# One-core transformer block in fp32: chunk 0 of the router sent through in the last attention slot, and the first two refinement steps reordered around it

## The reference, cut to what matters

```python
x = x + L0_xattn(layernorm(x), ctx)     # FFT autocorrelation, top-11 shifts, one row per sequence
x = x + L0_ffn(layernorm(x))            # 128 -> 512 -> 128, weights composed from 32 low-rank pairs
x = x + L1_xattn(layernorm(x), ctx)     # plain attention, one head of 128
x = x + L1_ffn(layernorm(x))            # router, 8 experts, 2 iterations

# L1_ffn, per token:
logits = gelu(x @ w_r1 + b_r1) @ w_r2 + b_r2          # router: top 2 of 8 experts
integrated, v = x, 0
for _ in range(2):
    ctx = [integrated, v]
    shared = inl(gelu(ctx @ w_s1 + b_s1) @ w_s2 + b_s2)      # alpha, beta, gate
    routed = weighted sum over the 2 experts of inl(gelu(ctx @ w1[e] + b1[e]) @ w2[e] + b2[e])
    x_next, v_next = sw * shared + (1 - sw) * routed
    halt = sigmoid(gelu(x_next @ w_h1 + b_h1) @ w_h2 + b_h2)
    refined = gelu(x_next @ w_f1 + b_f1) @ w_f2 + b_f2
    integrated += halt * refined * integration_weight
    v = v_next
```

## Time and profile before

| what | value |
|---|---|
| median of 3 runs | 349.97 us (349.29 to 350.16) |
| profiled execution | 348.92 us |
| its span, first to last instruction | 347.1 us |
| mean granted TensorE clock | 0.985 |
| TensorE busy | 317.9 us (92%) |
| VectorE busy | 263.5 us (76%) |
| ScalarE busy | 192.9 us (56%) |
| GpSimd busy | 36.5 us (11%) |

### The profile page before, as it was taken

The page is one execution under the profiler, slowest core; times in us unless marked ns, Lnnn a source line. Parts: engine busy times, 40 slices in busy tenths (PEclk is TensorE's granted clock), DMA queues, the critical chain, the costliest instruction groups (busy, mean ns, idle before and its releaser), DMA issues.

```text
span 347.1 us, 4339 instructions
## 1 busy us (share of the span) xinstructions
PE 317.9 (92%) x1482; PEld 224.9 (65%) x1490; DVE 263.5 (76%) x529; ACT 192.9 (56%) x303; POOL 36.5 (11%) x47
## 2 busy tenths in 40 slices
PE   4989999899899458899899999999999999999995
PEld 4764697555465336567576777767777777776763
DVE  1474844558656776798969988999996996999693
ACT  3410024366936643497877966777556746545743
POOL 0030012122020203103710020000000000000000
PEclk9989999999989899999999999999999999999999
DMA  7999940000000000015263154001001000000001
GB/s 265 428 423 293 313 190 0 0 3 1 0 2 0 0 1 2 0 60 136 48 181 60 62 144 85 16 0 32 0 0 28 5 0 1 32 0 20 12 0 60
DMA packets 13172, 25.20 MB, mean 73 GB/s; under 512 B 608, under 2 KB 9056, under 8 KB 11872
## 3 DMA queue, kind: packets, MB, share of 16 engines
q1 hardware_dynamic: 11712, 20.75, 16.7%
q0 software_dynamic: 1440, 4.19, 6.5%
HBM read 16.55 MB, written 1.05 MB: 51 GB/s over the span
## 4 chain that ended last, share of the span: by engine, by line
PE 74%; DVE 14%; ACT 6%; issue 4%; DMA 1%; DVEq 0%; ACTq 0%
PE ps L1346 70%; DVE ring L1014 1%; PE ps L1444 1%; ACT ring L533 1%; ACT L533 1%; DMA pA<-in_packA 1%; DVE st L801 1%; PE ps L1560 1%; PE ps L1463 1%; DVE wz L1014 1%; DVE a L817 1%; PE ps L1433 1%; DVE ring L948 1%; DVE xtok L1001 1%; DVE ring L956 1%
## 5 line engine op out<-in xcount | busy, mean ns | idle before, releaser
L1346 PE MATMUL ps<-hm_even,ew_hi 128*128 128x512 f32 (+1 forms) x152 | 48.6, 418 | 1.4 <-issue 1.4
L1346 PE MATMUL ps<-hm_odd,ew_hi 128*128 128x512 f32 (+1 forms) x148 | 47.1, 421 | 0.0
L1346 PEld LDWEIGHTS ps<-hm_even,ew_hi 128*128 128x128 f32 (+1 forms) x152 | 26.4, 188 | 6.4 <-issue 1.5
L585 ACT ACTIVATE hid<-ps,pB 128x512 f32<-128x512 f32 x32 | 21.7, 688 | 14.4 <-PE ps L1346 13.8
L1346 PEld LDWEIGHTS ps<-hm_odd,ew_hi 128*128 128x128 f32 (+1 forms) x148 | 25.6, 189 | 5.5 <-issue 0.5
L1346 PE MATMUL ps<-hm_even,ew_lo 128*128 128x512 f32 (+1 forms) x72 | 25.3, 392 | 0.0
L431 POOL TENSOR_TENSOR zz<-zz,mhalf 128x4 f32<-128x4 f32 x12 | 12.4, 1034 | 100.3 <-DVE zz L906 100.3
L1346 PE MATMUL ps<-x_hi,w1x_hi 128*128 128x512 f32 x40 | 18.8, 470 | 4.2 <-DVE xtok L1001 3.6
L1346 PE MATMUL ps<-hm_odd,ew_lo 128*128 128x512 f32 (+1 forms) x64 | 22.3, 394 | 0.0
L1014 DVE SCALAR_TENSOR_TENSOR ring<-ring,pB,hid 128x1024 f32<-128x1024 bf16 x16 | 20.5, 1282 | 0.8
L525 ACT ACTIVATE hB<-ps 128x512 f32<-128x512 f32 x16 | 9.6, 597 | 19.8 <-PE ps L1346 19.8
(11 more groups left out here) (324 smaller groups left out, 757.3 us busy)
## 6 DMA issues: line engine op xcount, KB each, us to landing
ring<-in_fc1b SPq DMA_DIRECT2D x4, 1024.0 KB, 17.2
ring<-in_fc2a SPq DMA_DIRECT2D x4, 1024.0 KB, 7.4
hm_odd<-hm_odd SPq DMA_DIRECT2D x4, 512.0 KB, 3.5
packC<-in_packC SPq DMA_DIRECT2D x1, 1152.0 KB, 9.1
pB<-in_packB SPq DMA_DIRECT2D x1, 1077.0 KB, 8.7
ctxT<-in_ctxT SPq DMA_DIRECT2D x2, 512.0 KB, 6.3
xtok<-in_xtok SPq DMA_DIRECT2D x1, 1024.0 KB, 8.7
xT<-in_xT SPq DMA_DIRECT2D x1, 1024.0 KB, 10.7
```

Of the source, the lines that this page charges most:

```text
L585: act.activation(hid[:, j, :], hid_bank(s, j), ACT.Gelu, bias=W("eb1", j, j + 1)).then_inc(sem("hid"), 1)
L1346: return pe.matmul(out, lhsT, rhs, start=start, stop=stop)
```

## The change

Nothing is added to or taken from the arithmetic: the same matmuls, masks and gelus are issued, in another order and partly in other banks. `route`, `second_exp` and `weigh` run three times (chunk 0; chunks 1 and 2; chunk 3) where they ran twice. In words:

- the splits of `w1x`, `wf1`, `wh1` and `wh2` move from slots 1 (ScalarE) and 2 (VectorE) to slot 0
- the router uses bank 4, that of the feed-forward, in place of bank 7, so `scores` waits for no logits any more; `router1` and `router2` of a slot stand behind its scores
- in slot 3 the route of chunk 0 is worked out and expanded, and three of its hidden tiles are computed; the state's high half for steps 0 and 1 is copied by ScalarE instead of VectorE
- the rest of the last chunk's attention, the router of chunk 2, `expand(1)`, and all of chunk 3's norm and router go between tiles of BETA and GATE of step 0
- all tiles of `hidden(1)` use bank 7, so each waits for the gelu of the one ahead
- `expand_weights(0)` and `expand(2)` go behind GATE of step 0, `hidden(2)` into BETA of step 1, and `weights_1` behind it
- `second_exp(3, 1)` stands between `squashed(1, BETA)` and `refine1(0)`

```diff
@@ banks
-            return (bank[7], bank[7], bank[4], bank[1])[c]
+            return (bank[4], bank[4], bank[0], bank[6])[c]
...
+        def routed(c):
+
+            return (1, 2, 2, 3)[c]
@@ gpsimd
+                if n == LN["att", 3]:
+                    pool.wait_ge(sem("minus_1"), 1)
+                    pool.wait_ge(sem("share"), 1)
+                    weigh(0, 1)
             for n, s in enumerate(MOVED):
...
                 if s == 1:
-                    weigh(2)
+                    weigh(1, 2)
+                if s == 2:
+                    weigh(3, 1)
@@ scalar
+            act.activation(w1x_hi, pB[:, colB["ew1"][1]:colB["ew1"][1] + W1C], ACT.Copy)\
+                .then_inc(sem("w1x_hi"), 1)
             gelus(0, (2, 3))
...
+            for t in range(NCH):
+                a, q = t >= 1, t >= 2
+                if t:
+                    gelus(t, range(FT))
+                if a:
+                    exps(t - 1)
+                if t == 1:
+                    act.activation(swc[:, 0:1], W("sw"), ACT.Exp, scale=-1.0).then_inc(sem("swe"), 1)
+                if t == 3:
+                    second_exp(0, 1)
+                if q:
+                    center_evac(t - 2)
+                if t == 2:
+                    r1_gelu(0)
...
+                    state_high(0)
+
+            act.wait_ge(sem("consts"), 4)
+            expand_evac(0, 2, 3)
+            hidden_gelus(0, (1, 3))
+            r1_gelu(1)
+            hidden_gelus(0, (0,))
+            exps(3)
+            center_evac(2)
+            hidden_gelus(0, (2, HT))
+            state_high(1)
+            r1_gelu(2)
+            squashed(0, BETA)
+            expand_evac(1, 7, 6)
+            hidden_gelus(1, (1,))
+            center_evac(3)
+            hidden_gelus(1, (0, 2))
+            r1_gelu(3)
+            hidden_gelus(1, (3, HT))
+            weights_evac(0, 7, 6)
+            expand_evac(2, 7, 6)
+            state_high(2)
+            squashed(0, GATE)
+            second_exp(1, 2)
...
                 squashed(s, BETA)
+                if s == 1:
+                    second_exp(3, 1)
                 refine1(s - 1)
@@ vector
                 if s == 1:
                     kept(s, 2)
                     high(s, 2)
+                    ln_scale("rt", 3)
                     lower(s, 1)
                     kept(s, 3)
                     high(s, 3)
+                    logits(3)
                     lower(s, 0)
                     state_split(s + 1)
                     slot_masks(s + 1)
                     shared_halves(s)
+                    route(3, 1)
...
+                if t == 3:
+                    state_split(0)
+                    route(0, 1)
+                if a:
+                    att_norm(t - 1)
                 if q:
                     ln_scale("rt", t - 2)
...
+            kept(0, 1)
             att_scores(3)
             att_max(3)
+            att_add(2)
+            logits(1)
+            lower(0, 1)
             ln_stats("rt", 2)
+            kept(0, 3)
+            att_norm(3)
+            lower(0, 3)
+            att_pt(3)
             ln_scale("rt", 2)
             kept(0, 2)
             lower(0, 2)
+            lower(0, 0)
+            shared_halves(0)
             att_add(3)
             logits(2)
+            route(1, 2)
+            state_split(1)
             ln_stats("rt", 3)
             slot_masks(1)
             kept(1, 1)
@@ tensor, slots
                 ffn_down(t, (0, 1))
                 if q:
                     ln_spread("rt", t - 2)
-                ffn_down(t, (2, 3))
+                ffn_down(t, (2,))
+                if t == 3:
+                    pe.wait_ge(sem("fh"), FT * NCH)
+                    expand(0, 2, 3)
+                ffn_down(t, (3,))
...
+                if t == 3:
+                    hidden(0, (1,))
+                if a:
+                    probs_t(t - 1)
+                ln_tok("att", t, "x2")
+                scores(t)
+                if t == 3:
+                    hidden(0, (3,))
                 if q:
                     router1(t - 2)
                 if a:
-                    probs_t(t - 1)
+                    att_v(t - 1)
+                if t == 3:
+                    hidden(0, (0,))
                 if q:
                     router2(t - 2)
 
             ln_tok("rt", 2, "x3")
             center(2)
+            hidden(0, (2, HT))
             ln_spread("rt", 2)
@@ tensor, steps 0 and 1
-                    controls(0, BETA, between={5: next_hidden})
-                    controls(0, GATE, between={2: weights_0, 4: expand_2})
+                    controls(0, BETA, between={5: attended, 3: valued})
+                    controls(0, GATE, between={2: expand_1, 3: hidden_1, 4: hidden_0, 5: hidden_2, 6: hidden_3})
+                    router2(3)
+                    hidden(1, (HT,))
...
+                    expand_weights(0, 7, 6)
+                    pe.wait_ge(sem("cb"), 2)
+                    expand(2, 7, 6)
...
-                controls(s, BETA, between={1: {5: hidden_rest, 6: expand_3, 13: weights_1},
+                controls(s, BETA, between={1: {3: hidden_first, 5: hidden_rest, 13: expand_3},
                                            2: {3: hidden_rest, 5: weights_2, 6: weights_3}}.get(s, {}))
+                if s == 1:
+                    weights_1()
```

More of the change, by code:

```diff
@@ L265, in hid_bank @@
             if s <= 1:
-                return bank[((2, 3), (7, 6))[s][order(s).index(j) % 2]]
+                return bank[((2, 3), (7, 7))[s][order(s).index(j) % 2]]
             return bank[(6, 7)[j % 2]]
         def order(s):
-            return {0: (1, 2, 0, 3, HT), 1: (1, 0, 2, 3, HT)}.get(s, tuple(range(HT + 1)))
+            return {0: (1, 3, 0, 2, HT), 1: (1, 0, 2, 3, HT)}.get(s, tuple(range(HT + 1)))
         def hid_at(s, j):
@@ L727, in last_halt @@
                     .then_inc(sem("lth"), 1)
-            act.wait_ge(sem("consts"), 4)
-            for s in range(STEPS):
-                if s == 0:
-                    squashed(0, BETA)
-                    state_high(2)
-                    second_exp(2)
-                    weights_evac(0, 7, 6)
-                    expand_evac(2, 7, 6)
-                    squashed(0, GATE)
-                    continue
+            for s in range(1, STEPS):
                 if s + 1 < STEPS:
@@ L897, in ln_stats @@
                 n = LN[which, c]
[L898 removed]
+                t = tok_bank(n)
                 dve.wait_ge(sem("tok_ps"), n + 1)
@@ L1196, in _ @@
+            shared_halves(0)
             att_add(3)
             logits(2)
+            route(1, 2)
+            state_split(1)
             ln_stats("rt", 3)
-            state_split(1)
-            ln_scale("rt", 3)
             slot_masks(1)
-            lower(0, 0)
-            kept(0, 3)
-            lower(0, 3)
-            shared_halves(0)
             kept(1, 1)
-            logits(3)
-            route(2)
             dve.wait_ge(sem("consts"), 4)
@@ L1523, in att_v @@
                     b = c * BPC + j
-                    last = mm(bank[5][:, j * S:(j + 1) * S], vtok[:, b, :], pT[:, c % 2, j, :])
+                    last = mm(att_bank(c)[:, j * S:(j + 1) * S], vtok[:, b, :], pT[:, c % 2, j, :])
                 last.then_inc(sem("o_ps"), 1)
@@ L1746, in controls @@
                 late = s == 1 and rows_last
-                for i in (1, 3, 5, 2, 4, 6) if n == LAST else range(1, NT):
+                for i in (1, 3, 5, 2, 4, 6) if n == LAST else (1, 2, 5, 6, 3, 4) if n == 0 else range(1, NT):
                     if i in between:
```

319 lines of the change are left out of this document (149 added, 170 removed).

## The result

The changed kernel takes 353.8 us (median of 6 runs, 351.8 to 354.13) beside 350.07 for the kernel before (6 runs, 349.29 to 351.24): a ratio of 1.0097, with a 95% interval of 1.0068 to 1.0125. Slower by 3.7 us or 1%, where a gain of 0.8 us was forecast (349.2). The kernel before spreads more than its first three runs showed: 31 executions beside e1 lie between 348.67 and 351.24. The profiled execution took 353.62 us, with a span of 351.8 beside 347.1.

What follows compares the result with a forecast made beforehand. TensorE was taken as the bound, busy 92% of the span with 74% of the chain. Terms -6.7 + 3.0 + 1.7 + 1.2 = -0.8 us gave 348.1 on the profiled execution, 349.2 on the median; range 346.3 to 351.9.

Steps and rivals of the forecast that it cites:

- Slot 0, nothing: Slot 0: the moved weight splits fit into VectorE's rest and ScalarE's copies into its waits for TensorE, so they cost nothing.
- Slot 2, -2.9: Slot 2: scores stop waiting for logits; 1.6 + 0.2 us rest and 1.5 slow clock go, some 0.4 comes back; gain 2.9.
- The new rests, 11.5, and 1.7 for the powers: Slot 3 to refine_a(0): TensorE's new rests total 11.5 us, gaining 3.8 there; GpSimd's held powers add 1.7.
- two thirds of the rests come back: Slot 3 to refine_a(0): the prediction's remark that two thirds of the rests return in other places.
- halt_a, +3.0: Halting head, step 1: halt_a(0) waits for refine1(0)'s gelu, delayed by second_exp(3, 1) with its table load; cost 3.0 us.
- The powers, +1.7: GpSimd's powers for scores(3) and chunk 2's norm: each held some 0.9 us by VectorE's kept(0,1) and kept(0,3); cost 1.7.
- The weights on GpSimd, 0: weigh(1, 2) and weigh(3, 1) on GpSimd end before weights_1 and weights_3; cost between 0 and 0.5 us, taken as 0.
- Clock, +1.2 for one drop: Two new rests of 2.7 to 2.9 us might lower TensorE's clock; one drop charged at 1.2 us, range 0 to 3.6.
- an even chance: Odds of a clock drop at each new rest of 2.7 to 2.9 us: 3.13 brought 1.2 GHz, about 2 did not.
- Rival B: Chunk 2's norm to expand(2): clock falls at every long rest, three drops cost 3.6 us; +1.6, 351.6 us; chance 0.20.
- two large ones: Kernel before: TensorE's rests for chunk 0's logits (1.57 us) and the route of chunks 0 and 1 (3.13), both followed by half clock.

Runs made afterwards that it cites:

- e1: Changed kernel with 37 filler matmuls, whose results nobody reads, in its long rests, no wait changed: 348.23 us, ratio 0.9951 to the kernel before.
- e9: Kernel before with only the weight splits in slot 0 and the router in bank 4 behind the scores; tail and steps as before: 347.41 us, ratio 0.9934.
- e2: Changed kernel with GpSimd's two powers kept clear of VectorE's masking (kept(0, 1) behind logits(1), kept(0, 3) waiting for the power): 352.18 us, ratio 1.0068.
- e3: Changed kernel with second_exp(3, 1) moved from ahead of the halting head's gelu to behind halt1(0): 352.82 us, ratio 1.0084 to the kernel before.
- e6: Changed kernel with only eight filler matmuls, ahead of the spread of chunk 2's routing norm: 351.26 us, ratio 1.0032 to the kernel before.
- e7: Changed kernel with route(3, 1) ahead of state_split(2) and second_exp(3, 1) directly behind second_exp(1, 2), under one table load: 348.77 us, ratio 0.9986.
- e10: Changed kernel with added products at about 62 us that only move the rest of the program later: 355.08 us, ratio 1.0170 to the kernel before.
- e5: Changed kernel with ln_scale(rt, 3) on VectorE ahead of kept(1, 2) and high(1, 2): 346.26 us, ratio 0.9935 to the kernel before.
- e12: Kernel before with weight splits in slot 0, router in bank 4 behind the scores, and ten filler products ahead of expand(0): 344.66 us, ratio 0.9855.
- e4: Kernel before with filler in its two long rests, 6 matmuls ahead of scores(2) and 10 ahead of expand(0): 346.89 us, ratio 0.9927.

## Why the prediction was wrong, step by step

- **Slot 0, nothing.** Right: slot 2 starts at 81.95 instead of 81.88, and 0.06 of that is there in the setup already.
- **Slot 2, -2.9.** Right: the rest of 1.57 is gone and slot 3 starts 2.6 us earlier. e9 shows these two parts alone to be a gain, 2.3 in its median.
- **The new rests, 11.5, and 1.7 for the powers.** Right: 13.2 were laid out, 13.1 are in the window. Most single ones too: 2.78 at router1(3) for 2.9, 1.04 at chunk 3's transposes for 1.0, 1.41 and 0.69 around expand_weights(0) for 1.4 and 0.6. The one of 1.4 at hidden(2, 0) is not there; that the slow products ahead of it cover it is likely and not shown. That two thirds of the rests come back is a slip that the sum does not use: 11.5 of 14.1 us are four fifths.
- **halt_a, +3.0.** Right: 3.13, by the load and the exponential of L567.
- **The powers, +1.7.** Right in kind and near in size: 1.99 and 2.50 us instead of 1.9 each. The second ran beside three VectorE operations: kept(0, 3), the attention norm's product 0.13 us behind it, and a copy, at whose end (120.24) it ends (120.27). Which of them held it is not separated. Kept clear, both powers take 1.0 and the spread comes 1.0 us sooner (e2).
- **The weights on GpSimd, 0.** Right: TensorE has no rest there that GpSimd ends.
- **Clock, +1.2 for one drop.** This is the step that failed. There were three, and they cost 6.7 us in the profiled execution: busy time over the 59.3 + 6.6 of the two stages at full clock (64.23 + 8.39). The other terms, as measured, sum to -0.8 - 1.2 + 0.3 (slot 2) - 0.1 (rests) + 0.1 (halt_a) = -1.7, and 348.92 - 1.7 + 6.7 = 353.9 beside 353.62. Filler in the rests alone, which keeps the clock full, takes 5.6 off the median (e1). Two assumptions were wrong in it. The number: "an even chance" for each rest of nearly 3 us took the length of the single rest as what decides. The clock fell behind the same rest of 2.78 at router1(3) in e3, e6, e7 and e10, and not in the changed kernel's profile. And the price: 1.2 was six slowed products in a stretch of 3.4 us whose first part lay in a rest; two of the new ones last 6.8, and all but the first 1.2 us of the first lies on work, most of it control tiles. It costs some 2.6 more than the 3.4 us ahead of the spread do (e5, e10). What decides whether and where the clock falls stays open.

Rival B, with a chance of 0.20, had the right mechanism and the right number of drops, and two of the three at its place; the third, at halt_a, lies behind it. That the count came out is in part luck: B tied the drops to the long rests, and of those over 2.5 us the one at router1(3) had none in this profile, while a stretch began inside the rest of 1.41 at expand_weights(0). The time was 2.2 us over its 351.6 by the price: three at 1.2 are 3.6, and they cost 6.7. Two of its readings were too kind. Not only the second drop beyond the one in the sum takes the total over zero, the first does (-0.8 + 1.2). And the rows held a sign against the length as what decides: the clock fell behind a rest of 1.57 us and not behind the one of about 2, which is 2.03 in the timeline (at 130.41) and so larger than one of the "two large ones".

By the Trainium skill (TensorE: Matmul & The Clock Gate, Part 1) the slow clock is the default and activity releases it. The traces agree as far as they go: from BETA of step 0 to refine_a(0) the changed kernel rests 8.7 us instead of 4.1 and its clock falls twice there in part or whole, and with 37 idle products more (e1) not once. But from slot 3 to refine_a(0) as a whole it rests less than before (13.1 beside 14.1 us) and has 13.7 us at half clock instead of 3.4. So the amount of rest alone does not give the price either.

## What to carry to other kernels

When a change moves rests into a stretch that was full, price the clock with them. Look at what work stands behind each rest, and for each slow stretch charge up to half of its length; count on more than one. A rest that can't be removed can be filled with products that nobody reads, where a bank is free; here 10 of them in one rest of 3.5 us were worth 2.7 us between the medians (e9 less e12) and took nothing from the path. It is no sure cure: in e4 the clock fell behind the next rest in four of ten executions, or so its profile and the mean clocks of the others suggest. And before an order is judged by its time, look at whether its slow stretches lie on work or beside a wait.

## What was not expected of the hardware

- A stretch at half clock is not of one length: 3.4 us (before, and the third of after), 6.8 (the first two of after), 10.2 (e9).
- The setup, the same in all kernels up to there, took up to 1.8 us longer by its own slow stretch (39.49 us in e2, 41.26 in e1, at the same product).
- The same instructions with the same waits had the clock fall at 115.3 us in one kernel's profile (e5) and at 119.2 in another's (after), and executions of one program were 3.7 us apart, the slower ones at a lower mean clock (e5).
- A rest's own length does not tell whether the clock falls: it did not behind 2.78 us (after) and 3.15 us (e5, at halt_a), it did behind the same two rests in e6 and e10, and it did near one of 1.03 us (e5, at 114.15).
- A GpSimd operation of 1.01 us took 2.50 where VectorE operations over SBUF inputs ran nearly back to back (after, at 117.77).
